# A Macaron block (experts, state space, experts) on one core: who sends the expert weights, where the shared tiles stand, and where the last router is computed

## What is computed

```python
x = x + 0.5 * ffn(layernorm(x))      # routed + shared experts
x = x + mamba(layernorm(x))          # selective scan over 256 steps, 16 states
x = x + 0.5 * ffn(layernorm(x))      # the same experts once more

def ffn(x):
    scores = sigmoid(x @ w_router.T)
    w, i = top_k(scores, 2);  w = w / w.sum()
    out = sum over the two experts e in i of w[e] * ((silu(x @ wg[e].T) * (x @ wu[e].T)) @ wd[e].T)
    out += sum over j in 0, 1 of (silu(x @ sg[j].T) * (x @ su[j].T)) @ sd[j].T
```

## Time and profile before

| | |
|---|---|
| median of 3 runs | 531.88 us (531.19 to 533.93) |
| the profiled execution, its own time | 529.17 us |
| its span in the trace | 527.2 us |
| PE clock granted | 0.998 of full speed |
| last matmul in the trace ends | 520.3 us |
| PE without a matmul ahead of that | about 12 us |

### The profile page before, as it was taken

The page is one execution under the profiler, slowest core; times in us unless marked ns, Lnnn a source line. Parts: engine busy times, 40 slices in busy tenths (PEclk is TensorE's granted clock), DMA queues, the critical chain, the costliest instruction groups (busy, mean ns, idle before and its releaser), DMA issues.

```text
span 527.2 us, 11153 instructions
## 1 busy us (share of the span) xinstructions
PE 508.2 (96%) x4410; PEld 414.2 (79%) x4411; DVE 324.4 (62%) x658; ACT 158.6 (30%) x337; POOL 231.4 (44%) x208
## 2 busy tenths in 40 slices
PE   8999988989999999999998999999999999999994
PEld 6989975448988999546897799974489999974684
DVE  3742423721665999997679489999966732521224
ACT  1111122222037444545211644445521111212210
POOL 1050100140512999998335289999930352000022
PEclk9999999999999999999999999999999999999999
DMA  7956994860305455551221444555300132210012
GB/s 236 388 225 250 402 396 170 262 219 22 98 14 135 111 117 154 139 144 52 68 84 63 99 127 131 130 155 139 90 22 3 40 111 61 73 47 23 21 52 80
DMA packets 42230, 67.88 MB, mean 129 GB/s; under 512 B 5152, under 2 KB 24992, under 8 KB 42176
## 3 DMA queue, kind: packets, MB, share of 16 engines
q1 hardware_dynamic: 29424, 38.94, 26.0%
q10 hardware_dynamic: 9088, 18.09, 9.2%
q0 software_dynamic: 3664, 10.10, 5.9%
HBM read 48.89 MB, written 18.22 MB: 127 GB/s over the span
## 4 chain that ended last, share of the span: by engine, by line
PE 77%; DVE 8%; DMA 7%; issue 3%; POOL 2%; ACTq 1%; ACT 1%; another core or an unknown queue 1%; POOLq 0%; SPq 0%; DVEq 0%
PE ps L515 33%; PE ps L540 16%; PE ps L530 14%; PE ps L553 7%; DMA w_gu<-in_wu 3%; PE ps L559 2%; PE ps L564 2%; ACTq L810 1%; DMA region<-yg_rows,ypos 1%; DVE xres L1187 1%; PE ps L703 1%; DMA bcb<-bc_rows 1%; DVE hb L1027 1%; POOL region L971 1%; DMA xres<-in_x 1%
## 5 line engine op out<-in xcount | busy, mean ns | idle before, releaser
L515 PEld LDWEIGHTS ps<-xt,w_gu 128*128 128x128 f32 x1400 | 161.6, 192 | 9.4 <-issue 6.4
L515 PE MATMUL ps<-xt,w_gu 128*128 128x128 f32 x1400 | 164.2, 276 | 3.6 <-ACT xt L794 2.4
L1027 DVE SCALAR_TENSOR_TENSOR hb<-hb,ps 128x640 f32<-128x640 f32 x68 | 55.5, 816 | 123.2 <-ACT hb L776 113.8
L540 PE MATMUL ps<-w_dn,hb 128*128 128x256 f32 x520 | 120.7, 379 | 0.0
L540 PEld LDWEIGHTS ps<-w_dn,hb 128*128 128x128 f32 x520 | 94.8, 190 | 10.8
L776 ACT ACTIVATE hb<-ps 128x640 f32<-128x640 f32 x68 | 47.6, 700 | 180.7 <-PE ps L515 152.0
L1072 DVE TENSOR_TENSOR_SCAN ps<-ps,region 128x512 f32<-128x512 f32 x64 | 78.3, 1223 | 8.0 <-ACT ps L867 4.9
L515 PE MATMUL ps<-xnt,w_gu 128*128 128x128 f32 x680 | 80.8, 276 | 2.1 <-DVE xres L1042 2.0
L1005 POOL TENSOR_TENSOR xnt<-xnt,hh 128x512 f32<-128x512 f32 x64 | 81.7, 1278 | 2.5 <-DVE hh L1077 2.5
L515 PEld LDWEIGHTS ps<-xnt,w_gu 128*128 128x128 f32 x680 | 78.8, 192 | 4.5 <-DVE xres L1042 2.4
L530 PE MATMUL ps<-w_gu,xt 128*32 128x512 f32 (+2 forms) x768 | 74.6, 524 | 3.0 <-issue 3.0
(11 more groups left out here) (112 smaller groups left out, 320.7 us busy)
## 6 DMA issues: line engine op xcount, KB each, us to landing
bcb<-bc_rows SPq DMA_DIRECT2D x22, 512.0 KB, 5.1
region<-bc_rows SPq DMA_DIRECT2D x10, 512.0 KB, 5.1
xg<-xg_rows SPq DMA_DIRECT2D x35, 128.0 KB
w_gu<-in_wg ACTq DMA_DIRECT2D x7, 640.0 KB, 12.1
w_gu<-in_wu ACTq DMA_DIRECT2D x7, 640.0 KB, 13.3
w_dn<-in_wd ACTq DMA_DIRECT2D x7, 640.0 KB, 14.6
yg_rows<-ob SPq DMA_DIRECT2D x20, 128.0 KB, 3.5
xg_rows<-bcb SPq DMA_DIRECT2D x1, 2176.0 KB, 14.7
```

The source lines that it names most:

```text
L515: last = nc.tensor.matmul(gup(p)[:, c * P:(c + 1) * P], w_gu4[:, e, k, c * P:(c + 1) * P], x, start=(k == 0), stop=(k == KC - 1))
L540: ins = nc.tensor.matmul(outp(p), hb[:, p, c * P:(c + 1) * P], w_dn4[:, e, c, :], start=(c == 0), stop=(c == IC - 1))
L1027: nc.vector.scalar_tensor_tensor(out=h, in0=h, scalar=1.0, in1=gup(p)[:, 0:I], op0=ALU.add, op1=ALU.mult).then_inc(s_a, 1)
```

## The change

Four edits, in one diff.

1. **Weights.** Experts 1 to 4 are now sent by POOL (12 DMAs), right behind the second part of segment 0's scatter; experts 5, 6 and 7 by ACT (three DMAs each), in the middle of tiles 5, 6 and 7, behind the tanh and ahead of the copy of the next rows. Nothing is sent after tiles 3 to 6.
2. **Table.** The four DVE operations that fill `table` and `limit` leave `route_rows` and become a step of their own, `table`, placed later. PE's read of the table waits for them.
3. **Shared tiles.** Segment 3 now has four shared tiles ahead of the routed ones and four behind them (it had five and three).
4. **Schedule.** In segment 0 the second norm and all routing of segment 1 stand one tile earlier. At the start of segment 2, half of the combine of segment 1 is put ahead of `route_rows`, and PE's count (`R2`) goes right behind the down product of tile 32. For the last router (segment 3) the transposes of the normalised rows go between pieces 4 and 5 of tile 50's gate and up (`normed`), its logits behind that tile's last piece, their turn behind the down product of tile 49 (`logits`), and the count behind the whole gate and up of tile 51 (`ranked behind`).

```diff
           SHARED[0] + SHARED[1][:2] + ROUTED + SHARED[1][2:],
-          SHARED[0] + SHARED[1][:1] + ROUTED + SHARED[1][1:]]
+          SHARED[0] + ROUTED + SHARED[1]]
...
-    ("second", 0), ("tiles", 1, 6), ("N1", "P", 1), ("N2", "P", 1), ("tiles", 6, 8), ("T", "P", 1), ("tiles", 8, 9), ("R1", 1),
-    ("scored", 9, 1), ("second", 9), ("ranked", 10, 1), ("decay",), ("S", 1, 0), ("S", 1, 1),
-    ("second", 10), ("tiles", 11, S1 - 3), ("O", 0), ("G", 0),
+    ("second", 0), ("table", 0), ("tiles", 1, 5), ("N1", "P", 1), ("N2", "P", 1), ("tiles", 5, 7), ("T", "P", 1),
+    ("tiles", 7, 8), ("R1", 1), ("scored", 8, 1), ("second", 8), ("ranked", 9, 1), ("decay",), ("table", 1),
+    ("S", 1, 0), ("S", 1, 1), ("second", 9), ("tiles", 10, S1 - 3), ("O", 0), ("G", 0),
...
-    ("first", S2 + 15), ("T", "P", 3), ("second", S2 + 15), ("O", 2), ("R1", 3),
-    ("scored", S2 + 16, 3), ("second", S2 + 16), ("ranked", S3, 3), ("S", 3, 0), ("S", 3, 1), ("G", 2),
-    ("second", S3), ("tiles", S3 + 1, S3 + 7), ("C", 2, 0, TT), ("tiles", S3 + 7, S3 + 14), ("O", 3), ("G", 3),
-    ("tiles", S3 + 14, TILES - 1), ("C", 3, 0, 2), ("first", TILES - 1), ("C", 3, 2, TT), ("second", TILES - 1),
+    ("O", 2), ("normed", S2 + 15, 3), ("second", S2 + 15), ("logits", 3), ("ranked behind", S2 + 16, 3), ("S", 3, 0),
+    ("S", 3, 1), ("G", 2), ("second", S2 + 16), ("table", 3), ("tiles", S3, S3 + 6), ("C", 2, 0, TT),
+    ("tiles", S3 + 6, S3 + 13), ("O", 3), ("G", 3), ("tiles", S3 + 13, TILES - 2), ("C", 3, 0, 2), ("first", TILES - 2),
+    ("C", 3, 2, TT), ("second", TILES - 2), ("tiles", TILES - 1, TILES),
...
-        LATE = {3: (1, 2), 4: (3, 4), 5: (5, 6), 6: (7,)}
+        LATE = {}
+        LATE_MID = {5: (5,), 6: (6,), 7: (7,)}
+        BY_GPSIMD = (1, 2, 3, 4)
...
             def free_expert(s, group):
+                pe.wait_ge(s_pos, s + 1)
...
+                if norm is not None:
+                    turn_norm(("P", norm))
                 if kind_of(n) == "mixed":
...
                 rest_of_gate_up(n + 1)
+                if norm is not None:
+                    score(norm)
+                if ranks_behind is not None:
+                    rank(ranks_behind)
...
                     if n > 0:
                         act.wait_ge(s_dn, n)
                     tanh(n + 1)
+                for e in LATE_MID.get(n, ()):
+                    send_weights(e)
...
+                    if s == 0 and part == 1:
+                        for e in BY_GPSIMD:
+                            for k, (dst, src) in enumerate(weights_of(e)):
+                                pool.dma_start(dst, src).then_inc(s_w[e][k], 16)
```

More of the change, by code:

```diff
@@ L614, in turn_logits, with turn_norm, first @@
                 held[:] = [(s_neg, s + 1)]
-            def first(n, router=None, ranks=None):
+            def turn_norm(which):
+                k = NORM[which]
+                banks_free()
+                for t in range(TT):
+                    pe.wait_ge(s_xn, TT * k + t + 1)
+                    for d in range(KC):
+                        at = (t // 2 * 4 + d * 2 + t % 2) * P
+                        last = nc.tensor.transpose(both_banks[:, at:at + P],
+                                                   xn[which[0]][:, t, d * P:(d + 1) * P], ident[:, :])
+                    if t % 2 == 1:
+                        last.then_inc(s_xnp, 1)
+                held[:] = [(s_xnt, 2 * (k + 1))]
+            def first(n, router=None, ranks=None, norm=None, ranks_behind=None):
                 q = n % 2
@@ L757, in _ @@
                     first(step[1], ranks=step[2])
+                elif kind == "R2":
+                    rank(step[1])
+                elif kind == "normed":
+                    first(step[1], norm=step[2])
+                elif kind == "logits":
+                    turn_logits(step[1])
+                elif kind == "ranked behind":
+                    first(step[1], ranks_behind=step[2])
                 elif kind == "second":
@@ L872, in exponentials, with copy_norm @@
                 nc.scalar.activation(ex[:, :, :], ex[:, :, :], ACT.Exp).then_inc(s_ex, 1)
+            def copy_norm(which):
+                for b in range(2):
+                    act.wait_ge(s_xnp, 2 * NORM[which] + b + 1)
+                    ins = nc.scalar.activation(xnt[:, :, b * 2 * P:(b + 1) * 2 * P],
+                                               state_banks[:, b, :].rearrange("p (d t) -> p d t", d=KC), ACT.Copy)
+                    ins.then_inc(s_xnt, 1)
             nc.scalar.preload_act_table_set("exp_and_others")
@@ L912, in _ @@
                     first(step[1])
-                elif kind == "ranked":
+                elif kind in ("ranked", "ranked behind"):
                     first(step[1])
+                elif kind == "normed":
+                    copy_norm(("P", step[2]))
+                    first(step[1])
+                elif kind == "logits":
+                    exponentials(step[1])
                 elif kind == "second":
```

41 lines of the change are left out of this document (20 added, 21 removed).

## The result

| | before | after |
|---|---|---|
| median | 530.87 us (528.84 to 533.93, 14 runs) | 535.39 us (534.67 to 537.68, 14 runs) |
| ratio | | 1.0087, 95% interval 1.0069 to 1.0106 |
| span of the profiled execution | 527.2 us | 532.9 us |
| granted clock, mean | 0.998 | 0.993 |

The changed kernel is slower by 0.9%, 4.5 us; 527.9 and "faster" were forecast, and the time lies 4 us above the range. The two traces differ by 5.7 us.

The account below looks back on a forecast made before the run. PE was taken as the bound, busy 508.2 of 527.2 us, so only idle time could move. Segment 0's 4.3 + 0 - 3.9 + 3.6 = 4.0 us gain took the median from 531.88 to 527.9, range 524.0 to 531.3.

Parts of the forecast that it names:

- table: Segment 0: four table operations leave the path ahead of tile 1's hidden state and tile 0's eviction; gain 1.0 us.
- first rows from DRAM: Segment 0: new wait for tile 5's rows, SP's load sharing DMA engines with POOL's weights; loss 1.0 us.
- ACT's issue and the weights: Segment 0: ACT's 4.82 us DMA issue goes, gain 2.4; up weights land earlier for the first mixed tile, gain 1.9.
- start of segment 2: New wait of 0.8 us for the count, eviction waits shift; net 0, bounds -1.0 and +1.8.
- start of segment 3: Last router: 2.6 us lost waiting for the norm, 1.3 for tile 50's eviction; together 3.9, bounds 2.5 and 5.
- end: One more shared tile behind the routed ones: span ends 3.3 us behind the last matmul instead of 6.9; gain 3.6.
- bound of 3.0: Upper bound in us on the first rows' loss; stores landed in 3.0 at best, 5.8 at the median, 2.8 more.
- the load passes the backlog: Argument against late first rows: engines go round queues a packet at a time, so the wait stays near 1.0 us.
- POOL was not held up: Answers a rival, chance 0.10: POOL's 12 weight issues delay the second norm's power; 531.0, or 538 at twice issue time.
- The rival drawn from the Trainium skill: GpSimd's descriptor writing starves while DVE is in a fast mode, holding up POOL's weight issues; 531.0, within chance 0.10.
- the first rows come late: Rival, chance 0.17: POOL's backlog delays tile 5's load, wait 3.0 us instead of 1.0; 529.8.

Follow-up runs that it names:

- weights edit alone: The kernel before with edit 1 (experts 1 to 4 sent by POOL, 5 to 7 by ACT in mid-tile) and nothing else: ratio 1.0034.
- the traces with fillers: Changed kernel or variants with useless identity matmuls in PE's waits; changed kernel with both waits filled, rows by 4.6 us: ratio 1.0013.
- the changed kernel's other trace: The changed kernel run once more, nothing altered, on another set of runs: ratio 1.0070 to before.
- one expert early, start of segment 2 as before: Changed kernel with expert 1 sent between scatter parts, experts 2 to 4 after the first rows, segment 3 and start of segment 2 as before: ratio 0.9911.
- weights as before: Changed kernel with the weights sent by ACT after tiles 3 to 6 as before, all other edits kept: ratio 1.0043.

## Why the prediction was wrong, point by point

Shifts against before, from PE's timeline; minus is a gain.

| step | forecast | measured |
|---|---|---|
| table | -1.0 | -1.0 at 28 us, but given back at the rows |
| first rows from DRAM | +1.0 | +5.3, and +1.7 by the clock |
| ACT's issue and the weights | -2.4 - 1.9 | -4.4 |
| start of segment 2 | 0 | +0.2 |
| scan of segment 2's half | not named | +0.7 |
| start of segment 3 | +3.9 | +5.9: waits 3.6, clock 1.5 in this execution, the rest in small pieces |
| end | -3.6 | -2.7 |
| sum | -4.0 | +5.7 |

**The step that failed is "Segment 0, the first rows from DRAM".** The mechanism was named, POOL's DMAs ahead of SP's load in the same engines, but sized at 1.0 with a bound of 3.0, and it measured 5.2 of wait, of which some 4.1 are the weights' (6.2 us from the issue to PE's going on, for 2.1 alone). The step said that "only one or two weight DMAs are ahead at 40.6, not a full backlog". It took POOL's issues at the pitch of its scatter, 1.26 us; they came at 0.66. At 41.4 two were out, and within the 2.1 us that the load needs alone three more, against engines that move 399 GB/s, 640 KB in 1.6 us. And the bound of 3.0 was a difference of stores at best and median in one stretch, where the backlog may already delay the best; the bound should have been the 5.8 beside a load alone, 3.7 us. Another 0.8 of the 5.2 us is that the row load was issued later, 41.41 for 40.61, as the second part of the scatter waited longer for the first: its last DMA stands at 38.94 for 38.15. It stands at 38.31 in the run with the weights edit alone, and at 39.39 with everything but that, so this does not come from the weights but goes with the table's move, as shown above; the step "Segment 0, the table" had it at a gain of 1.0 and no cost.

By the Trainium skill, "DMA: Bandwidth & Descriptors", the section on queues, rings and completion order, I said that the load passes the backlog, as each engine goes round its queues a packet at a time, and that the wait stays near 1.0. The runs do not bear that out: the load took 2.1 us alone and 6.3 with POOL's twelve around it. What failed is my inference; no run here shows how the engines take turns.

**The clock was in no step.** Idle PE time was priced at its own length. Behind both new waits of the compared trace the granted clock fell to 0.50 and cost 1.7 and 1.5 us more; the traces with fillers show it at both places. That is 3.2 of the 9.7 us of the miss; the second part of it came in four of the six profiled executions that have this wait unfilled. The trace of before gave no hint: its gap of 2.40 us lies in a stretch at a clock of 1.00.

**Right**: ACT's issues (0.55 to 0.77 us for 4.82) and the weights (2.00 to 0), 4.4 for 4.3. POOL was not held up: its issues took 0.66 us where I feared more, and it was free 13.37 us ahead of the power. The rival drawn from the Trainium skill, "SBUF — State Buffer", summary of rules, that descriptor writing starves beside DVE, shows in no issue of the weights here. The waits of segment 3 were right in kind and size, 2.22 and 1.33.

**Mis-sized**: the tail, 4.2 us for 3.3. The last eviction was on time (529.17, 0.5 behind the matmul); the last store of 128 KB was issued at 529.19 and took 3.3 us to land where before it took 2.5. The 0.7 us ahead of the scan of segment 2's half was not named; the changed kernel's other trace shows 0.46 of wait there for 0.81, and I have not run it down. And the table's gain, right where it was looked for, was worth nothing at the next wait: with a load of 2.1 us the rows were ready before only some 0.6 us ahead of PE (an estimate, 40.61 + 2.1 for 43.28), and the table's move made them later besides.

The rival "the first rows come late" was the case, but a third of the size: it put 2.0 us on top of the forecast, and the place cost 6.0 on top of it (5.3 + 1.7 - 1.0). Its 529.8 would still have been faster than before. That the wait and the clock's price come together was missed.

## What to carry to other kernels

- Before a stream is moved ahead, ask which small transfer on the path is issued in the next few microseconds, and price it behind the stream at the issue pitch of plain DMAs (0.66 us for 640 KB here), not alone. The cure was the order: one expert where POOL stood idle, the rest when the first rows were in. By itself it turned 1.0070 to 1.0087 into 0.9957; with segment 3 as before as well it is 0.990.
- Put a price on PE's idle time above its length: behind 3.7 to 7.5 us it cost another 1.6 us or more each time, behind 2.2 us in four profiled executions of six. A filler matmul in the idle time shows this price, and is worth trying where the wait can't be moved; it must end ahead of what is waited for.
- A gain is worth what is left of it at the next wait that it doesn't move: undo each edit of a bundle by itself and look there.

## What the runs showed of the hardware

- The clock does not follow from the length of the idle time alone. The changed kernel waited 2.22 us for the norm in both of its traces, and the clock fell in one and stayed in the other. It fell behind 2.02 (one expert early, start of segment 2 as before), but not behind 1.79 and 1.48 at the same place, and not behind 2.40 in the kernel before or 2.06 with the weights as before, where ACT's copy was waited for. What sets it is open. The Trainium skill, "TensorE: Matmul & The Clock Gate", part 1 on the clock gate, gives the levels 1.2 and 2.4 GHz; the traces agree, with 0.50 and 1.00.
- POOL issued a plain DMA of 640 KB in 0.55 to 0.77 us, an indirect one in 0.97 at a pitch of 1.27.
- The first load of 128 KB took 2.1 us alone, and 6.3 to 6.8 with POOL's weights queued around it, the ones behind it up to 8.4; with ACT's six sent beside the second part of the scatter, its small writes took 6.1 us for 2.4.
- Moving four DVE operations of 1.0 us behind an eviction went with a scatter whose first part landed 0.4 to 0.9 us later in sixteen of the seventeen traces that have it, and 1.2 in the other; the reason is open.
